# Reciprocals of the softmax sums broadcast into the free half of the attention accumulator, and the x1 transposes moved one tile later

## The reference

```python
# layer 0, part A
qkv = x @ W_qkv.T + b_qkv;  q, k, v = split(qkv, 3)
kv_state = cumsum(k * v, axis=tokens)
g = sigmoid(x @ W_gate.T + b_gate)
x = layernorm(x + q * kv_state * g)                     # x1
# part B: two transformer layers, 8 heads of 64, window 512
x1 = x
for l in (0, 1):
    h = shift_token(x)
    q, k, v = split(h @ wqkv[l], 3);  q, k = rotary_xpos(l2norm(q) * qs, l2norm(k) * ks)
    sim = where(mask, -inf, 8 * q @ k.T)                # own and previous window of 512 keys
    o = softmax(sim) @ v
    x = x + o @ wo[l]
    h = layernorm(shift_token(x)) * lg + lb
    a, g = split(h @ w1[l] + b1[l], 2)
    x = x + (a * gelu(g)) @ w2[l] + b2[l]
out = layernorm(x1 + x)
```

## Time and profile before

| | us |
|---|---|
| time, median of 2 runs (3809.73 and 3812.83) | 3811.28 |
| the profiled execution's own time | 3843.99 |
| its span, core 1, the slowest of 8 | 3842.4 |
| spans of the 8 cores | 3773.3 to 3842.4 |
| busy: TensorE matmul / VectorE / ScalarE / GpSimd | 2621.2 / 1569.4 / 562.4 / 516.6 |
| attention over heads, layer 0 and layer 1 | about 590 each |

### The profile page before, as it was taken

How to read it: one execution, slowest core, us unless ns; L and a number is a source line. 1 busy time by engine, 2 the same in 40 slices (tenths; PEclk the granted TensorE clock), 3 DMA queues, 4 the chain that set the end, 5 groups by cost and what they waited for, 6 DMA issues and landing times.

```text
span 3842.4 us, 34745 instructions; the slowest of 8 cores (3773.3 to 3842.4 us)
## 1 busy us (share of the span) xinstructions
PE 2621.2 (68%) x10044; PEld 955.0 (25%) x10044; DVE 1569.4 (41%) x2609; ACT 562.4 (15%) x862; POOL 516.6 (13%) x933
## 2 busy tenths in 40 slices
PE   2567894656767764489899746667767536998970
PEld 1312331221211111133333312211211202443430
DVE  2685563664344334321221346534344423222216
ACT  0011121111221211211011011121211121111001
POOL 3000001000000003043333000000000032344210
PEclk9987997775555558599988867655555757999985
DMA  7200002000000003485576010000000074566622
GB/s 102 33 1 6 17 14 52 1 1 1 1 1 1 1 12 48 60 112 74 73 89 73 16 29 1 1 0 1 1 1 1 12 103 66 73 96 91 91 53 88
DMA packets 136870, 143.12 MB, mean 37 GB/s; under 512 B 33436, under 2 KB 115356, under 8 KB 136688
## 3 DMA queue, kind: packets, MB, share of 16 engines
q0 software_dynamic: 129632, 128.01, 23.8%
q1 hardware_dynamic: 7056, 12.88, 1.0%
HBM read 249.90 MB, written 12.58 MB: 68 GB/s over the span
## 4 chain that ended last, share of the span: by engine, by line
PE 49%; DVE 26%; issue 8%; DMA 7%; ACT 5%; POOL 3%; DVEq 1%; ACTq 0%; SPq 0%; POOLq 0%
PE pA L1041 6%; PE pG L1046 6%; PE pP L281 5%; DVE stat L664 4%; PE pX3a L1097 4%; PE pX3b L1097 4%; PE pAV L711 4%; DMA W1g<-w_i 3%; DVE g2f L302 3%; PE pST L731 2%; PE pST L728 2%; PE pWo L814 1%; DMA wst<-Wqkv 1%; PE pS L731 1%; PE pS L728 1%
## 5 line engine op out<-in xcount | busy, mean ns | idle before, releaser
L1041 PE MATMUL pA<-HN,W1a 128*128 128x512 bf16 (+1 forms) x1408 | 360.6, 402 | 86.6 <-DMA W1g<-w_i 55.6
L1065 DVE SCALAR_TENSOR_TENSOR HG<-pA,b1ac,scr 128x512 bf16<-128x512 f32 (+1 forms) x176 | 132.1, 750 | 582.7 <-ACT scr L1060 582.7
L1046 PE MATMUL pG<-HN,W1g 128*128 128x512 bf16 (+1 forms) x1408 | 349.9, 393 | 0.0
L1023 POOL DMA_DIRECT2D W1a<-w_i x384 | 237.8, 619 | 720.3 <-PE pG L1046 718.3
L1060 ACT ACTIVATE scr<-pG,b1gc 128x512 bf16<-128x512 f32 (+1 forms) x176 | 120.9, 687 | 865.0 <-PE pG L1046 865.0
L1027 POOL DMA_DIRECT2D W1g<-w_i x384 | 240.6, 626 | 29.5 <-issue 29.4
L512 PE MATMUL pQKV<-AQ,XT 128*128 128x512 bf16 x768 | 228.2, 468 | 8.6 <-DVE rope L486 8.6
L751 DVE TENSOR_TENSOR APT<-APT,m 128x128 bf16<-128x128 bf16 x256 | 57.7, 226 | 418.8 <-ACT APT L747 418.8
L797 POOL DMA_DIRECT2D AO<-wo_i x8 | 4.3, 561 | 1593.5 <-DVE AoT L782 1593.5
L1041 PEld LDWEIGHTS pA<-HN,W1a 128*128 128x128 bf16 (+1 forms) x1408 | 140.9, 102 | 277.6 <-issue 148.1
L281 PE MATMUL pP<-WqkvT,XT 128*128 128x512 bf16 x768 | 189.6, 391 | 0.0
(11 more groups left out here) (224 smaller groups left out, 3282.6 us busy)
## 6 DMA issues: line engine op xcount, KB each, us to landing
W1a<-w_i POOLq DMA_DIRECT2D x320, 128.0 KB, 7.2
W1g<-w_i POOLq DMA_DIRECT2D x320, 128.0 KB, 7.5
W2i<-w_i POOLq DMA_DIRECT2D x42, 256.0 KB, 17.7
wst<-Wqkv POOLq DMA_DIRECT2D x24, 256.0 KB, 4.2
AQ<-wqkv_i POOLq DMA_DIRECT2D x16, 384.0 KB, 16.5
XS<-x POOLq DMA_DIRECT2D x16, 256.0 KB, 15.2
x1h<-XS SPq DMA_DIRECT2D x16, 256.0 KB, 2.0
out<-of_sb SPq DMA_DIRECT2D x8, 512.0 KB, 3.1
```

The costliest lines, as they stand in the source:

```text
L1023: E("ge", lambda e, j=j, b5=b5, wa=wa, l=l, bb=bb: e.dma_start(out=W1a[bb][:, 512 * j:512 * j + wa], in_=self.dw1[l, 128 * j:128 * (j + 1) ...
L1041: ins = e.matmul(pA[pp][0:wh, :], W1a[bb][:, 512 * j + 128 * i5:512 * j + 128 * i5 + wh], HNc[:, 512 * j:512 * (j + 1)], start=(j == 0), s ...
L1046: ins = e.matmul(pG[pp][0:wh, :], W1g[bb][:, 512 * j + 128 * i5:512 * j + 128 * i5 + wh], HNc[:, 512 * j:512 * (j + 1)], start=(j == 0), s ...
L1065: E("ve", lambda e, wh=wh, pc=pcglob, pp=pp: e.scalar_tensor_tensor(HG[0:wh, 512 * pc:512 * (pc + 1)], pA[pp][0:wh, :], b1ac[0:wh, pc:pc + ...
```

## The change

Four edits. First, in the loop of `phase_WA` tile t-2 is transposed in step t instead of tile t-1, the waits on `pP3` follow, and two tiles are left to transpose behind the loop. Second, `pAV` is declared with 128 partitions (the same banks). Third, a head's end: the row of reciprocals is spread over `pAV[64:128]` instead of over `pS` and `pST`, and the roles of copy and multiply change: VectorE first copies the numerators `pAV[0:64]` to `AoT`, then multiplies `AoT` in place by `pAV[64:128]`. The TensorE products of the four chunks wait for ScalarE's reciprocals alone. `Arbc` is gone. Fourth, the first two score tiles of a head wait for the last exponential of the head before instead of for its last multiply.

```diff
-            if t >= 2:
-                w = [("ve", ve_ext[t - 2])]
-            elif t == 1:
-                w = [("ve", ve_kv[0])]
+            if t >= 3:
+                w = [("ve", ve_ext[t - 3])]
+            elif t > 0:
+                w = [("ve", ve_kv[t - 1])]
...
-            if t > 0:
-                ve_ext[t - 1] = self.transpose_tile_to_xt(
-                    t - 1, pP3, [("ve", ve_x1[t - 1]), ("ve", ve_kv[t])])
+            if t > 1:
+                ve_ext[t - 2] = self.transpose_tile_to_xt(
+                    t - 2, pP3, [("ve", ve_x1[t - 2]), ("ve", ve_kv[t])])
...
+        ve_ext[NT - 2] = self.transpose_tile_to_xt(
+            NT - 2, pP3, [("ve", ve_x1[NT - 2]), ("ve", ve_ext[NT - 3])])
         ve_ext[NT - 1] = self.transpose_tile_to_xt(
-            NT - 1, pP3, [("ve", ve_x1[NT - 1])])
+            NT - 1, pP3, [("ve", ve_x1[NT - 1]), ("ve", ve_ext[NT - 2])])
...
-        Arbc = [self.sb(stM, f"Arbc{i}" + L, [64, 512]) for i in range(2)]
...
-        pAV = self.ps(stP2, "pAV" + L, [65, 2048])
+        pAV = self.ps(stP2, "pAV" + L, [128, 2048])
...
                 elif h > 0:
-                    w.append(("ve", ve_oT[h - 1]))
+                    w.append(("se", se_exp[(h - 1, NT - 1)]))
...
             for qc in range(4):
-                rb = pS if qc % 2 == 0 else pST
-                w = [("se", se_r)]
-                w.append(("ve", C["ve"]))
-                E("pe", lambda e, qc=qc, rb=rb: e.matmul(
-                    rb[0:64, 0:512], self.cones[0:1, 0:64],
+                E("ve", lambda e, qc=qc, g=g, base=base: e.tensor_copy(
+                    AoT[base:base + 64, 2048 * g + 512 * qc:2048 * g + 512 * (qc + 1)],
+                    pAV[0:64, 512 * qc:512 * (qc + 1)]),
+                  wait=[("pe", pe_av_done)])
+                E("pe", lambda e, qc=qc: e.matmul(
+                    pAV[64:128, 512 * qc:512 * (qc + 1)], self.cones[0:1, 0:64],
                     rwb[0:1, 512 * qc:512 * (qc + 1)], start=True, stop=True),
-                  wait=w, inc=[("pe", 1)])
+                  wait=[("se", se_r)], inc=[("pe", 1)])
                 pe_rbc[qc] = C["pe"]
-                E("ve", lambda e, qc=qc, rb=rb: e.tensor_copy(Arbc[qc % 2][:],
-                                                             rb[0:64, 0:512]),
-                  wait=[("pe", pe_rbc[qc])])
                 E("ve", lambda e, qc=qc, g=g, base=base: e.tensor_tensor(
                     AoT[base:base + 64, 2048 * g + 512 * qc:2048 * g + 512 * (qc + 1)],
-                    pAV[0:64, 512 * qc:512 * (qc + 1)], Arbc[qc % 2][:], op=OP.mult))
+                    AoT[base:base + 64, 2048 * g + 512 * qc:2048 * g + 512 * (qc + 1)],
+                    pAV[64:128, 512 * qc:512 * (qc + 1)], op=OP.mult),
+                  wait=[("pe", pe_rbc[qc])])
```

## The result

The changed kernel takes 3762.4 us, the median of 11 runs, beside 3841.0 for 10 runs of the kernel before. The ratio is 0.9858 with a 95% interval of 0.9823 to 0.9893. Taken off the 3811.3 us of the forecast's base, that is 54 us less (41 to 67), where 57.7 were forecast.

A forecast was written before the change was run, and what follows sets the result against it. No single engine bounds the kernel; a head's end is a chain of short steps waiting for each other. Heads' ends -51.5, early scores -6.6, transposes +0.4 give -57.7 us off the median 3811.28: 3753.6 us, range 3730 to 3785.

The forecast's parts named there:

- The freed spreads: At each head's end, spreads wait for ScalarE alone; three VectorE gaps of 0.92 us shrink to 0.11, 2.43 us less.
- The copy that hides: At each head's end, the first copy runs under ScalarE's two instructions; 0.79 us less.
- The early scores: At 14 head starts, the first reduction follows the last multiply after 0.11 instead of 0.58 us; 6.6 us less.
- The multiply: At a head's end, the multiply with new operands was to stay at 684 ns.
- slow-multiply rival: At a head's end, each multiply costs 3.28 instead of 0.68 us, total 3920 us; chance 0.03.
- the bound from all-SBUF operands: Lower bound for the multiply at a head's end: 426 ns, 16.5 us more gain, 3737 us in total.
- Two readers of one bank: Logarithm and first copy share banks at a head's end; 11 us less gain if in turn, nothing taken.
- The transposes: In phase_WA: 0.96 us less in step 1, 1.34 us more behind step 15, net +0.4 us.
- All four copies hidden: Rival at a head's end: VectorE runs copies 1 to 3 early, 38 us more gain, 3716 us; chance 0.01.
- Pass 2 stayed at half clock: Judges the rival that pass 2 of each head runs at full clock, saving up to 281 us, about 3470; chance 0.02.
- The clock in the feed-forward phases: Rival: earlier feed-forward phases meet a better TensorE clock, 31 us more gain, 3722 us; chance 0.13; the other way 3785.
- Two per cent are 76 us: Whole kernel: taken as what measurement can tell from no change, line at 3735 us; faster 0.15, same 0.82, slower 0.03.

The follow-up runs named there:

- e6: The changed kernel with the old roles of copy and multiply (reciprocals copied to SBUF), spreads still free of VectorE; 3785.8 us in one run.
- e3: The changed kernel, but a head's first two score tiles wait for the last multiply again; 3734.6 us in one run.
- e5: The changed kernel with all four copies of the numerators ahead of the first multiply; ratio 0.9784 to the kernel before.
- e11: The kernel before with only the transposes moved one tile later, run a second time; 3857.1 us in one run.
- e4: The kernel before, unchanged, profiled once more; 3789.9 us in one run.
- e9: The changed kernel timed and profiled again; ratio 0.9858 (0.9805 to 0.9912) to the kernel before.
- e8: The changed kernel with ScalarE's logarithm and exponential in halves, one copy instead of four, multiplies 1024, 512 and 512 wide; ratio 0.9722 to the kernel before.
- e1: The kernel before with only the transposes moved one tile later; 3866.9 us, median of 6, beside 3853.5 for the kernel before.
- e10: The kernel of e8 timed and profiled again; ratio 0.9691 to the kernel before, median 3684 us.

## Why the forecast was right, and where it was not

**The sum.** Forecast 58.1 us less in attention, measured 60.2 in the heads alone, 58.1 by phases (29.6 and 28.5), and 54 (41 to 67) for the whole program by the timed ratio, beside 57.7. The mechanism held. Its parts, each with its run:

- *The freed spreads* (forecast 2.43 us per head's end). e6 against the kernel before: 9.68 to 7.14 us, 2.54. Of all terms this one is off by most: 0.1 us at each of 16 heads' ends, 1.8 us. The spread starts 0.15 instead of 0.25 us behind ScalarE's end; the prediction left the 0.25 as it was. Shown by e6's timeline. That the missing second wait is the reason is argued, not shown.
- *The copy that hides* (0.79). e6 against the changed kernel: 7.14 to 6.35, 0.79. Shown.
- *The early scores* (0.47 x 14 = 6.6). e3: 6.4 by phases, 6.9 in the heads alone. Shown.
- *The multiply* kept at 684 ns is 691, which costs 0.4 us in all; so the sign named for it ("must stand at 684 ns") was missed by 7 ns. The slow-multiply rival, with 3.28 us, and the bound from all-SBUF operands, with 426 ns, are both gone.
- *Two readers of one bank*: the logarithm is 1869 ns beside copies as it was without. The price is nothing, the lower bound. The trace agrees with the rule of the Trainium skill, "PSUM — Partial Sum Buffer", section "PSUM bank collisions raise a hardware error", for one bank in different 32-partition groups: the logarithm reads partition 64 and the copies read partitions 0 to 63. e5 shows it for four copies in a row.
- *The transposes* (+0.4): the end is +1.32 as worked out, but the loop gives back 0.5 to 0.6 us instead of 0.96 at the same clock, so the term is +0.8. What the term left out is TensorE's clock in the first steps: the time at 0.50 is shorter there with the move, which brings the end of `phase_WA` to 610.4 us from 612.1 on average (e11).

**The rivals.** All four copies hidden was rightly excluded for this order and is real in the other (e5). Pass 2 stayed at half clock: the changed kernel's window from 900 to 916, TensorE busy 15.77 of 16 us, is granted 0.50. The three idle stretches of each head's end are gone and the clock stayed where it was, so they were not what held it down; the 4.2 us in which TensorE waits for ScalarE are still there. The trace still disagrees with the Trainium skill, "TensorE: Matmul & The Clock Gate", section "Part 1: The HAM clock gate", by which a busy array is given its full clock.

```profile
900.00:916.00 16.00, 15.77 (x43) 4.25 (x42) 3.38 (x15) 5.25 (x10) 0.00 (x0) 0.50 0.00 1
```

The clock in the feed-forward phases moves an execution by tens of microseconds, as the earlier trace rows had it, but for the kernel before as well (e4 against the first trace), so it is scatter on both sides and no effect of the change.

**The step that failed** is the one that turned the sum into chances: "Two per cent are 76 us, about what a measurement of this kernel can tell from no change". It is the size of the scatter that was wrong, and with it the forecast of "same" with a chance of 0.82 for a sum that said 1.5% less. The measured interval reaches 13 us to either side of 54 (41 to 67), and that of e9 20 us; both exclude no change clearly, and in the heads alone the 60 us stand against a scatter of 0.4. The prediction gave no row for its 76 us, and the two numbers that it had were smaller: 33 us between the profiled execution and the median, 3 us between the two timed runs. A change of 1.5%, worked out term by term, had to be told as a gain. The place of each term and the total held. That the timed 54 us lie within 4 us of the forecast is partly luck, with an interval of 13 us to either side.

## What to carry to other kernels

Where three engines hand a small piece of work round a loop, each of them is idle for a good part of each round: in a round of 2.40 us TensorE worked 0.60 and VectorE 1.36. Let the producer run ahead into space that is already allocated (here the unused half of the accumulator's partitions), and put everything that doesn't depend on the late operand ahead of the first instruction that waits for it. By phases, reordering alone (e5) brought another 37 us and pipelining the slow row computation in halves (e8) 20 more. Where single executions scatter by 1%, compare the phases between markers on every core: here the medians of attention agree within 2 us, and those of the heads within 0.1, where the spans of one program are 54 us apart (3842.4 and 3788.4). And tell a sum that is built this way as the change that it says, not by the scatter of single runs.

## What was not expected of the hardware

- Reading PSUM from partition 64 costs VectorE 7 to 10 ns more than from partition 0 (copy 693 against 683 ns, multiply 691 or 694 against 684), whatever the order of the inputs. The start partition is the reading that fits; it was not isolated.
- For stretches of mostly 100 to 200 us in the feed-forward phases two cores at a time, 0 and 1, 2 and 3, 4 and 5 or 6 and 7, are granted 0.81 of the clock, while other cores of the same die are not. In e1 and e11 there are longer ones, and some in `phase_WA`. In the first trace of the kernel before it was cores 0 and 1 from 1927 to 2089 us (0.80 and 0.82 in the window of 1900 to 2000, where cores 3 and 4 had 1.00 and 0.99) and cores 2 and 3 from 2043; in e4 and e10 no core was; in e8 cores 2 and 3 were from 3463 on, and cores 4 and 5 from 3468. The places change from one execution to the next of the same program, and what sets them off is not shown.
- In the first steps of the loop of `phase_WA` TensorE's clock falls to 0.50 and rises again, for 14 to 35 us in all. Each 6.7 us or so more at 0.50 makes the loop 3.1 us longer (the table under e11).
